# Graph units with two score slots of two PSUM banks, maxima in a slot of two banks and a slot of one, and softmax denominators laid out and spread by DMA

## The reference

```python
for c in range(NUM_NOD):                    # 6 nodes
    q = ew[c, 0] * (nodes[in_q] @ We[eq] + be[eq])
    k = ew[c, 1] * (nodes[in_k] @ We[ek] + be[ek])
    v = ew[c, 2] * (nodes[in_v] @ We[ev] + be[ev])
    o = _mha(q, k, v, Wq[c], Wk[c], Wv[c], Wo[c])   # 8 heads, softmax over 1024 keys
    nodes[c] = act_w[c] * o + q
out = _layernorm(nodes[5])
```

## Time and profile before

| what | value |
|---|---|
| median of 3 runs | 3509.16 us (3496.37 to 3542.75) |
| the profiled execution, its own time | 3483.55 us |
| its span | 3481.7 us |
| PE busy | 3058.8 us, 88% |
| DVE busy | 2517.9 us, 72% |
| ACT busy | 2290.9 us, 66% |
| POOL busy | 489.1 us, 14% |
| mean granted TensorE clock | 0.953 of full |

### The profile page before, as it was taken

The page is one execution under the profiler, slowest core; times in us unless marked ns, Lnnn a source line. Parts: engine busy times, 40 slices in busy tenths (PEclk is TensorE's granted clock), DMA queues, the critical chain, the costliest instruction groups (busy, mean ns, idle before and its releaser), DMA issues. The chain is left out here.

```text
span 3481.7 us, 46771 instructions
## 1 busy us (share of the span) xinstructions
PE 3058.8 (88%) x17215; PEld 1373.0 (39%) x17215; DVE 2517.9 (72%) x2916; ACT 2290.9 (66%) x3238; POOL 489.1 (14%) x392
## 2 busy tenths in 40 slices
PE   5699998999758999999999999999999999999994
PEld 4466665656413333333333333333333333333331
DVE  5756554555248888888888788878888888888853
ACT  1355665655515677777777677777777777777783
POOL 0211101111000011111111111111111111111103
PEclk9899999999858999999999899999999999999996
DMA  5000000000144343344334433433444334433402
GB/s 162 16 10 4 23 1 20 7 10 10 36 100 95 67 96 68 79 89 96 85 65 96 87 66 85 93 91 67 87 96 96 67 78 90 96 83 66 82 15 80
DMA packets 100143, 231.38 MB, mean 66 GB/s; under 512 B 18162, under 2 KB 54534, under 8 KB 96838
## 3 DMA queue, kind: packets, MB, share of 16 engines
q1 hardware_dynamic: 99334, 226.23, 28.5%
q10 hardware_dynamic: 576, 2.10, 0.2%
HBM read 152.94 MB, written 73.34 MB: 65 GB/s over the span
## 5 line engine op out<-in xcount | busy, mean ns | idle before, releaser
L1491 DVE TENSOR_REDUCE mx_b<-ps_max 128x2 f32<-128x1024 f32 x1536 | 1814.3, 1217 | 416.3 <-PE ps_max L1262 414.5
L1454 ACT ACTIVATE pt_b<-ps_pair 128x1024 f32<-128x1024 f32 x1079 | 1106.1, 1025 | 490.1 <-PE ps_pair L1276 489.0
L1328 PE MATMUL ps_ctx<-pt_b,vs 128*32 128x512 f32 x6144 | 838.0, 618 | 4.6 <-ACT c_b L1439 4.0
L1262 PE MATMUL ps_max<-ks,qs 48*128 48x512 f32 x3072 | 746.9, 433 | 53.5 <-DVE mx_b L1491 27.2
L1276 PE MATMUL ps_pair<-qs,ks 50*128 50x512 f32 x2158 | 544.8, 501 | 171.9 <-ACT pt_b L1454 168.8
L1276 PEld LDWEIGHTS ps_pair<-qs,ks 50*128 50x128 f32 x2158 | 203.7, 186 | 935.3 <-ACT pt_b L1454 524.8
L766 ACT ACTIVATE pt<-ps_pair,cb 128x512 f32<-128x512 f32 x470 | 313.1, 687 | 310.3 <-PE ps_pair L623 226.8
L1460 ACT ACTIVATE pt_b<-ps_misc 128x512 f32<-128x512 f32 x830 | 491.9, 593 | 2.0 <-PE ps_misc L1276 0.5
L1262 PEld LDWEIGHTS ps_max<-ks,qs 48*128 48x128 f32 x3072 | 377.1, 192 | 217.9 <-DVE mx_b L1491 133.8
L819 DVE TENSOR_REDUCE mx<-ps_max 128x2 f32<-128x1024 f32 x256 | 303.5, 1221 | 150.6 <-PE ps_max L595 88.4
L1276 PE MATMUL ps_misc<-qs,ks 50*128 50x512 f32 x830 | 340.1, 410 | 3.1 <-ACT part L1407 0.9
(11 more groups left out here) (151 smaller groups left out, 2420.3 us busy)
## 6 DMA issues: line engine op xcount, KB each, us to landing
partd<-part SPq DMA_DIRECT2D x24, 2048.0 KB, 6.4
qs<-partd SPq DMA_DIRECT2D x288, 128.0 KB, 5.7
ks<-partd SPq DMA_DIRECT2D x288, 128.0 KB, 6.7
xq<-node SPq DMA_DIRECT2D x24, 512.0 KB, 9.6
xk<-node SPq DMA_DIRECT2D x24, 512.0 KB, 10.5
xv<-node SPq DMA_DIRECT2D x24, 512.0 KB, 11.5
xf<-node SPq DMA_DIRECT2D x24, 512.0 KB, 4.2
node<-nt_b SPq DMA_DIRECT2D x48, 256.0 KB, 2.0
```

Source lines behind the costliest of these rows:

```text
L1262: ins = pe.matmul(psM[p % 2][:, CHUNK * odd:CHUNK * odd + CHUNK], qs[w % 2][rows, 2 * q + j, P * qb:P * qb + P], ks[w % 2][rows, 2 * q + j ...
L1328: ins = pe.matmul(psO[SLOT * i:SLOT * i + SLOT, :], vs[u % 2][:, kb, QUAD * (s // HALF_STEPS) + i], pt[:, entry(u, QUAD * s + i)], start=k ...
L1454: act.activation(pt[:, at:at + 2].rearrange("p k n -> p (k n)"), pair_bank(u, r)[:], ACT.Exp, scale=SCALE_B).then_inc(exp_done, 1)
L1491: nc.vector.tensor_reduce(mx2[:, kc, q, :, KB * j + qb], psM[p % 2][:].rearrange("p (h n) -> p h n", h=2), AX.X, ALU.max).then_inc(mx_done, 1)
```

## The change

Inside `graph` only. The PSUM slots are dealt anew: scores go in twos into `psM[0]` and `psM[1]` alternately (`bank`), and a round is now either one pair of scores or one other job, which takes the place of a pair in the same slot (`PLAN`, 73 rounds for most units). A round waits for the reader of the round two before it (`bank_free`). Maxima pieces use `psP` (two blocks) and `psX` (one block) alternately, sizes 2, 1, 2, 1 and so on (`SIZES`), 43 pieces to half a unit.

The denominators no longer go through VectorE's transposes, except in the last unit (`inverse_here`). SP does it (`denominators`): four transfers lay a row of 512 denominators of `c32` out over 32 partitions each (`den`), VectorE takes one reciprocal of 128 x 16 four rounds after the copy (`inverse`), one transfer writes the result to DRAM (`invd`), and after waiting for it four more spread it over 16 partitions each (`rec`). SP's order has these calls between the others, and both stores of unit `u-1` now stand in unit `u`. The subtraction `split` of the first projections moves from VectorE to POOL, the values from rounds 9 and 12 to 23 and 27, and projections, outputs and turns move likewise.

```diff
+        LAG = (6, 10)
+        PLAN = {2: ("turn", 0, 1), 9: ("output", -1, 0), 19: ("output", -1, 1), 23: ("values", 1, 0), 27: ("values", 1, 1),
+                31: ("project", 2, 0), 35: ("project", 2, 1), 39: ("project", 2, 2), 43: ("project", 2, 3),
+                60: ("turn", 1, 0)}
...
+        SIZES = []
+        for q in range(2):
+            while sum(SIZES) < BLOCKS * (q + 1):
+                SIZES.append(min(2 - len(SIZES) % 2, BLOCKS * (q + 1) - sum(SIZES)))
...
+        def steps_at(u, r):
+            since = filled(u, r) - (LAG[u == LAST] if r else LAG[0])
+            until = filled(u, r + 1) - LAG[u == LAST]
+            return range(max(0, since // QUAD), until // QUAD)
+        GROUP_ROUND = {BASE[u] + r: (S + 1) // KB - 1 for u in range(UNITS) for r in range(len(ROUND[u]))
+                       for S in steps_at(u, r) if S % KB == KB - 1}
...
+        def bank(u, r):
+            return (psM[0], psM[1], psP)[r % 3] if u == LAST else psM[r % 2]
...
+                def denominators(g):
+                    sp.wait_ge(o_copied, g + 1)
+                    for i in range(QUAD):
+                        at = SLOT * i + DV * (1 - g // NCHUNK % 2)
+                        sp.dma_start(den[SLOT * i:SLOT * i + SLOT],
+                                     c32[at:at + 1, g % 2].rearrange("o (p j) -> o p j", p=SLOT)).then_inc(den_in, D16)
+                    sp.wait_ge(inverted, g + 1)
+                    if g:
+                        sp.wait_ge(rec_in, REC * g)
+                    sp.dma_start(invd.rearrange("i (p j) -> (i p) j", p=SLOT), inv[:]).then_inc(inv_out, D16)
+                    sp.wait_ge(inv_out, D16 * (g + 1))
+                    if g:
+                        sp.wait_ge(cn_done, g)
+                    q = g // NCHUNK % 2
+                    for i in range(QUAD):
+                        at = SLOT * i + DV * q
+                        sp.dma_start(rec[q][at:at + DV], invd[i:i + 1].to_broadcast([DV, CHUNK])).then_inc(rec_in, D16)
...
                         load_values(u + 1)
-                    maxima_rows(u, 1)
                     if u:
+                        maxima_rows(u, 1)
+                        denominators(NG * u - 1)
+                        store(u - 1, 0)
                         store(u - 1, 1)
                     load_residual(u)
+                    if u < LAST:
+                        denominators(NG * u)
+                    if not u:
+                        maxima_rows(u, 1)
+                    if u < LAST:
+                        denominators(NG * u + 1)
                     if u < LAST - 1:
                         spill(u + 2)
                         stack(u + 2, 0)
                     if u < LAST:
+                        denominators(NG * u + 2)
                         maxima_rows(u + 1, 0)
-                    store(u, 0)
...
+                def inverse(g):
+                    dve.wait_ge(den_in, REC * (g + 1))
+                    if g:
+                        dve.wait_ge(inv_out, D16 * g)
+                    nc.vector.reciprocal(inv[:], den[:]).then_inc(inverted, 1)
...
+                    for r in range(len(ROUND[u])):
+                        for m in pieces_at(u, r, 0):
+                            maxima(*m)
+                        g = GROUP_ROUND.get(BASE[u] + r - 4)
+                        if g is not None and g < NG * LAST:
+                            inverse(g)
...
+                        for m in pieces_at(u, r, 1):
+                            maxima(*m)
```

More of the change, by code:

```diff
@@ L49 @@
 ENTRIES = 3 * QUAD
+BLOCKS = 2 * PIECES
 NODES = 6
@@ L1047, in graph @@
         MROWS = 4 * D16
-        AHEAD = PIECES + 4
+        REC = QUAD * D16
         LAST = UNITS - 1
[L1051 to L1071, removed]
@@ new lines, in graph, with rounds_of @@
+        FIRST_PLAN = {**PLAN, 28: ("turn", 0, 1)}
+        del FIRST_PLAN[2]
+        LAST_PLAN = {**PLAN, 63: ("output", 0, 0)}
+        def rounds_of(u):
+            plan = FIRST_PLAN if u == 0 else LAST_PLAN if u == LAST else PLAN
+            out, n = [], 0
+            while n < NS:
+                kind, ahead, k = plan.get(len(out), ("score", 0, n))
+                if not 0 <= u + ahead <= LAST:
+                    kind, ahead, k = "score", 0, n
+                out.append((kind, u + ahead, k))
+                if kind == "score":
+                    n += 2
+            return out
@@ L1099, in pieces_at @@
             if u == LAST:
                 return []
[L1101 to L1129, removed]
+            todo = ([(0, p) for p in range(AHEAD, NM)] if u == 0 else []) + [(u + 1, p) for p in range(NM)]
@@ L1232, in _ @@
                     unit(u)
+                store(LAST, 0)
                 store(LAST, 1)
@@ L1339, in unit @@
                 def unit(u):
-                    for r in range(ROUNDS[u]):
-                        pair(u, r)
-                        for w, p in pieces_at(u, r, 0):
-                            maxima(w, p)
-                        kind, w, k = single(u, r)
-                        if kind != "none":
-                            before = last_single(u, r)
-                            if before:
-                                single_free(*before)
-                            else:
-                                pe.wait_ge(mt_copied, 1)
+                    for r, (kind, w, k) in enumerate(ROUND[u]):
+                        bank_free(u, r)
+                        to = bank(u, r)
@@ L1376, in _ @@
-                    values(0, n)
+                    pe.wait_ge(pj_copied, n + 1)
+                    values(0, n, free[n])
                 for p in range(AHEAD):
@@ L1470, in unit @@
+                        g = GROUP_ROUND.get(BASE[u] + r)
                         if g is not None:
                             context_copy(g)
+                free = [psM[n % 2][:, CHUNK * (n // 2):CHUNK * (n // 2) + CHUNK] for n in range(PJ)]
                 for n in range(PJ):
-                    project(0, n)
+                    project(0, n, free[n])
                 act.wait_ge(ones, 1)
                 for n in range(2):
-                    values(0, n)
+                    values(0, n, free[n])
@@ L1514, in unit @@
-                def unit(u):
-                    for r in range(ROUNDS[u]):
-                        for w, p in pieces_at(u, r, 0):
-                            maxima(w, p)
-                        inverses(sum(ROUNDS[:u]) + r)
-                        for w, p in pieces_at(u, r, 1):
-                            maxima(w, p)
+                        both = mx2[:, BLOCKS * q:BLOCKS * q + BLOCKS].rearrange("p (n k h) -> p n k h", k=2, h=2)
+                        nc.vector.tensor_tensor(mx[:, PIECES * q:PIECES * q + PIECES].rearrange("p (h n) -> p n h", h=2),
+                                                both[:, :, 0], both[:, :, 1], ALU.max).then_inc(mx_final, 1)
@@ L1527, in _ @@
                 ins.then_inc(ones, 1)
-                for n in range(PJ):
-                    low_part(dve, nc.vector, 0, n)
                 for p in range(AHEAD):
@@ L1574, in unit @@
                     normalise(u, 2)
-                for n in range(PJ):
-                    low_part(pool, nc.gpsimd, 1, n)
+                for w in range(2):
+                    for n in range(PJ):
+                        split(w, n)
                 split_maxima(0, 0)
```

314 lines of the change are left out of this document (152 added, 162 removed).

## The result

The changed kernel takes **3891.62 us** (median of 4 runs, 3885.09 to 3897.18), 1.1126 times the time before, with a 95% interval of 1.1078 to 1.1174. The profiled execution took 3891.42 us, its span is 3889.6 us. The forecast, 3650, had the sign and the waits; the size lies outside the range.

What follows compares the result with a forecast made beforehand. No engine full; the one-slot `psP` loop between PE and ACT sets the pace. Forecast: 101 us plus 6.5 for the clock, 108 a unit against 99.4; 3482 + 181 - 9 = 3654, rounded to 3650 us; range 3420 to 3800.

Steps and rivals of the forecast that it cites:

- Part 4: Denominators by DMA: DVE waits in order for late transfers, PE and ACT stop too; 101 us a unit.
- the two waits: DVE ahead of reciprocals: 11 us for group 4u-1, 4 to 5 us for group 4u+2, each unit.
- the second rival: At `inverse(4u-1)` in round 7: small transfers aren't held up, unit 86 us, about 3190 us; chance 0.12.
- the place in SP's queue: Denominators issued at T = 11 to 13 stand behind stack and loads in SP's ring, landing at T = 19.2.
- reductions: DVE's maxima: 1.16 us per 1024 columns, 0.63 per 512; 76.4 us a unit against 74.2, 2.2 more.
- r = 1.18, a unit of 86 us: 73 rounds a unit at 1.18 us each if nothing else waited; -13 us per unit alone.
- The lower bound, 78 / 73 = 1.07: Shortest round in us, with DVE never idle: 78 us of DVE's work over 73 rounds a unit.
- the first episode: Granted clock falls to 0.50 after the unit's first stall idles PE about 10 us; costs 4 us.
- the half episode of the second wait: Second stall idles PE about 4 us, so half a slow-clock episode is counted; both together 6 to 7 us.
- The start: Values move to rounds 23 and 27, past the 4.98 us wait and its slow stretch: -9 us.
- The first (stalls cost little): Rival: stalls come without clock episodes, 97 to 101 us a unit, 3425 to 3510 us; chance 0.18.
- The third: Rival: clock stays low, three episodes and r = 1.25, 116 us a unit or more, 3830 us up; chance 0.12.

Runs made afterwards that it cites:

- E4: Changed kernel with SP's order altered: stack behind group 4u-1's denominators, spill ahead of spreading group 4u+1's inverses; 3484.14 us, 0.9938 of the time before.
- E8: Changed kernel with only the move at the unit's start: loads, maxima rows and group 4u-1's transfers before the stack; 3601.38 us, 1.0309 of the time before.
- E9: Changed kernel with only the move around the spill: spill goes out before group 4u+1's inverses are spread; 3777.43 us, 1.0812 of the time before.
- E2: Changed kernel with the four denominator lay-out transfers issued from ACT's queue right behind its copy, not SP's; 3956.37 us, 1.1348 of the time before.
- E1: Changed kernel with new slots kept, inverses back on VectorE's transposes and no denominator transfers by SP; 3538.84 us, 1.0147 of the time before.
- E6: E4 with VectorE reducing only half of each block of scores and the exponential's scale made smaller; 3366.51 us, 0.9651 of the time before.
- E3c: Changed kernel with 12 extra 128-row matmuls in round 9 of units 1 to 22, results overwritten; 3809.3 us, 1.0942 of the time before.
- E3: Changed kernel with 48 extra 50-row matmuls in round 9 of units 1 to 22, results overwritten; 3986.37 us, 1.1407 of the time before.
- E3b: Changed kernel with nine extra 128-row matmuls in round 9 of units 1 to 22, results overwritten; 3876.22 us, 1.1073 of the time before.
- E7: E4 with the maxima in three one-bank slots, a piece running up to two ahead of VectorE's; 3470.24 us, 0.9932 of the time before.

## Why the forecast was right in kind and too small

**Right: the place and the waits.** Part 4 held step by step. With T = 0 at the stack's first issue, DVE's wait ended at T = 20.9 (forecast 19.2), it lasted 11.8 us (11), PE resumed at T = 22.3 (20.7). Group 4u landed in 2.1 us, without a wait. DVE's waits sum to 16.6 us a unit (15 to 16). E4, E8 and E9 show by order of issue alone that the two waits are the loss. A landing unhindered by what was issued ahead of it, the second rival, is what E4 brings about, and not what the change did.

**Only in part: why the landing is late.** The prediction put it down to the place in SP's queue. The Trainium skill, "DMA: Bandwidth & Descriptors" (Queues, rings and completion order), has transfers from one issuing engine consumed in ring order; 8.4 us for 2 KB behind the stack and 2.1 us for the same transfers without it agree with that. But E2 has them on ACT's queue, where the stack doesn't stand ahead of them, and beside the same stack and loads they take 8.4 us again. So the place in the queue is not needed for the delay; bulk transfers in flight on the other queue are enough. Which of the two holds them back in after, no run tells apart. The numbers of Part 4 don't depend on it.

**Right: reductions.** 0.682 us for 512 columns and 1.218 for 1024 where 0.63 and 1.16 were taken back to back.

**Failed: "I take r = 1.18, a unit of 86 us".** Without the waits a unit takes 100.3 us (E1) or 98.6 - 2.4 = 96.2 (E4): r is 1.32 to 1.37. The lower bound, 78 / 73 = 1.07, was DVE's work alone; PE had no bound at all, though the earlier trace rows show it busy for 93 of 101 us. It should have had one, from the rows that I had. I read "two context steps are 1.07 us", but the row of 1.07 us has count 8, and the pages before and after count 6144 such records for 24 x 32 steps: eight to a **single** step. PE's timeline after, at the full clock, shows what that means:

```profile
2261.90 0.50 PE L1292 MATMUL ps_max<-qs,ks 50*128 50x512 f32 x2
2262.24 0.39 PE L1278 MATMUL ps_pair<-ks,qs 48*128 48x512 f32 x2
2262.47 0.40 PE L1292 MATMUL ps_max<-qs,ks 50*128 50x512 f32 x2
2262.71 0.40 PE L1278 MATMUL ps_misc<-ks,qs 48*128 48x512 f32 x1
2263.04 1.06 PE L1328 MATMUL ps_ctx<-pt_b,vs 128*32 128x512 f32 x8
2264.03 0.50 PE L1292 MATMUL ps_max<-qs,ks 50*128 50x512 f32 x2
```

Two pairs, three blocks of maxima and one step take 2.13 us without a gap. 32 times that is 68 us; the 32 blocks left over and the projections, values, outputs and turns come to some 18 more (an estimate from their rows, 0.2 us a block and 1 to 2 us a job). That is 86 us, again an estimate: 1.18 was **PE's sum without any gap**, which I took for a middle value. Before, a unit took 99.5 with PE nearly as full as in E1 and E4 (1740 of 1900 us, against 1764 and 1783), so better slots had little to give. That the slots and rounds bring nothing is shown by E1; that PE's work is why is argued, and why 10 us stay between PE's sum and the unit is shown only in part, by E6.

**The clock: near, partly by luck.** I counted 4 us for the first episode. E3c measures 3.3; the half episode of the second wait was not measured by itself. The episode is shorter than assumed (5 us after PE resumes, not 13.5), but it begins inside the wait.

**The sum by these values.** In the mean of 18 units after, PE resumes at T = 21.9 (forecast 20.7), the copy of group 4u+1 is over 48.2 us later (33.8 x 1.18 + 0.7 = 40.6), the reciprocal of 4u+2 starts 31.0 us behind it (29), and the unit ends 15.3 us later (1.5 + 7.8 x 1.18 = 10.7). The waits' own terms thus make 3.2 us. Rounds and clock make 12.2, where I had 6.5 for the clock and nothing for the rounds: the missing 5.7 us are 41.6 rounds at 1.32 instead of 1.18. With 1.37 they would be 7.9, and the clock 4.3. The failed step is 6 to 8 of the 8.4 us missed a unit; the waits, counted somewhat short, and the clock, counted well or somewhat high, make the rest.

**The start: missed by 46 us.** I put it at -9 and it is +36.8. The wait before `values` did go. But the clock stayed low without one. One stretch before, then after (columns as above):

```profile
1150.00:1200.00 50.00, 44.72 (x266) 16.72 (x266) 46.17 (x47) 32.81 (x45) 5.52 (x5) 1.00 0.40 83
```

```profile
1150.00:1200.00 50.00, 47.47 (x167) 16.72 (x163) 32.14 (x38) 20.36 (x22) 4.25 (x4) 0.50 0.36 80
```

PE is busier than before by the profile, at half the clock. It is the same in E4 (0.50) and passes earlier in E1 (0.78). It also differs between executions of the same instructions: up to round 9 of unit 1, E3, E3b and E3c are the changed kernel, and from unit 0's first load of `wv_b` to unit 1's they take 145, 171 and 145 us, and after 162. In E3c the clock is back at 1.00 by 1105 us, before any fill. What holds it down was not tried; it stays open, and part of the 46 us is chance.

**The rivals.** The first (stalls cost little) was wrong: 13 and 6 us a unit, by E9 and E8. The third came nearest in its number, 116 us and 3830 or more, but not by its reason: it wanted three episodes, and r = 1.25 was still too low.

## What to carry to other kernels

Give every engine its own sum before choosing a value between bounds, and count records against instructions first: a row's count may be two to an instruction. A small transfer on the path of the work can cost what is in flight ahead of it, from its own queue or from another, so order the issues by who waits for them. Another queue did not make the landing faster here, and cost a compute engine its issue time. Kernels E4 and E7, the change with the stack behind the denominators, are 11% faster than the changed kernel; against the kernel before (0.9938 and 0.9932, intervals below 1) they gain less than the 2% that the forecast called the least to be told from no change.

## What the hardware did that I had not expected

- **Four transfers of 2 KB take as long from another queue.** Beside the stack and the loads they landed 8.4 us after their issue from SP's queue (after) and 8.4 us from ACT's (E2); with little else in flight in 2.1 us (after) and 3.7 us (group 4u+2 of E2, the stack mostly through).
- **The clock fell under a busy PE.** 48 matmuls of 50 rows back to back, busy 3.00 of 3 us, ended at 0.54 and 0.50, while 12 of 128 rows kept 1.00 in the same place (E3, E3c). Halving the columns of the context products brought the mean from 0.97 to 0.80, and a kernel with less to do became 2.5% slower than its parent (1.0186 against 0.9938).
- **The clock can stay at 0.50 with no wait in sight**: PE busy 47.5 of 50 us over 1150 to 1200 us, in after and in E4.
- **Four issues from ACT take 2.4 us of ACT's time**, as they do of SP's (2.41 us), which computes nothing.
